# Attention one: layer-norm statistics and normalisation in four parts each, and the projections moved to later score banks

## The chip, the cores and the metric

The kernel runs on one core of one Trainium2 chip. The metric is the device time of one launch in microseconds (us).

## The reference

A two-layer tower over 8 x 1024 tokens with 256 channels: embedding, attention one, a mixture of four experts, a second attention, and a feed-forward layer quantised to four bits. The change touches attention one only:

```
h = h + attn(layernorm(h))
# attn, for each of 8 sequences of 1024 tokens and each of 16 heads of 16 channels
qkv  = x_head @ Wqkv + bqkv
att  = softmax((q @ k.T / 4) * tril(ones, -1))      # masked scores are 0, not -inf
out  = (att @ v) over all heads @ Wr + br
```

## The kernel before

Attention one (`attention_one`) takes the 8 sequences in two halves of 128 channels each, so 16 halves `hb`; a half has two groups (`gi` 0 and 1) of four heads. One turn of the loop is one half: a window of group 0 and a window of group 1. Each window computes 36 score banks (slots 0 to 35, event `S`): TensorE (PE) fills one of three PSUM banks `scoresT`, ScalarE (ACT) takes the exponential into `probs`, GpSimd (POOL) zeroes the masked triangle of some of them, and PE multiplies `probs` by `Vg` in six bursts (event `PV`, bursts 4 and 5 of a group run in the window after it).

All other work is hung on the slots by a table of positions, `AT[gi]`: `window()` puts each event behind a slot, and every engine walks the same list and runs what is its own. So the table sets the order of instructions on each in-order engine. The work that goes through PSUM uses a ring of four banks (`ring`): a use may be filled only when the use four places ahead of it has been read, by VectorE (DVE) or ACT (`bank_free`; for a pair of banks, both). The events are:

- `LN_STATS`, `LN_NORM`: DVE computes mean and variance of 8 token tiles (`st`, `mv`), POOL raises variance + eps to -1/2 (`rstd`, in `LN_NORM`), DVE writes the normalised `xn`. This is for the next half, once in a turn, in window 0.
- `XT`, `QK`, `MID`: PE transposes `xn`, ACT copies it (`xT`); PE projects to q and k in four banks; ACT reads each bank twice (`f32part`, and `parts` rounded to bf16), POOL subtracts, ACT copies the middle part (`MID`), POOL subtracts again (`parts_ok`). q and k are so split in three bf16 parts. In ACT's queue the copy of one `MID` stands ahead of the next `QK`.
- `V`, `VG`, `RSUM`, `SUF`, `TMP`, `EQ`, `PT`, `OM`, `OT`, `WR`: values, suffix sums for the masked part, division by the denominator, and the output projection, added to `h`.
- `MX`: the row maxima of the next group, 18 pairs of banks in a window. PE fills a pair, DVE reduces both. `CT` and the SP queue bring the result into `Qs`. The SP queue waits for `parts_ok` before it loads `Qm`, `Km` (`LOAD_MAX`) and then `stage` (`LOAD`).

Of the kernel before, what the change touches and what calls it, by code (L numbers as in the profile page):

```python
# [22 lines left out]
TPB = S // P  # L23
# [28 lines left out]
FUTURE = -2.0 ** 126  # L52
SCORE_BANKS, RING_BANKS = 3, 4
PROBS = 16


def score_slots():
# [20 lines left out]
def buffer(slot):  # L78

    return slot % PROBS if slot < 2 * PROBS else slot - 2 * PROBS + HPG  # L80

# [41 lines left out]
def wait_apart(eng, *waits):  # L123


    values = [value if isinstance(value, int) else eng.to_reg(value) for _, value in waits]
    if not all(isinstance(value, int) for value in values):
        eng.wait_ge(waits[0][0], 1)
    for (sem, _), value in zip(waits, values):
        eng.wait_ge(sem, value)  # L130
# [4 lines left out]


AT = {
    0: {"LN_STATS": 1, "LN_NORM": 3, "XT": 7, "PV_COPY": 4, "EQ": 6, "TMP": 0, "PT": 5, "OT": 24, "WR": 25, "RSUM": 5, "SUF": 12, "QK": (11, 13, 18, 20), "MID_LAG": 2, "V": 21, "VG": 5, "LOAD": 0, "MX": 2, "MX_END": 32, "MX_CURVE": 1.0, "PV_HALF": 14},
    1: {"PV_COPY": 4, "EQ": 6, "TMP": 0, "PT": 5, "WR": 1, "V": 8, "VG": 6, "LOAD": 0, "MX": 1, "MX_END": 32, "MX_CURVE": 1.0, "PV_HALF": 14},
    "V_IN": 0, "WR_IN": 1,  # L140
}
ALONE = {"LN_STATS": 0, "LN_NORM": 1, "XT": 2, "QK": (8, 9, 10, 11), "MID_LAG": 1, "V": 12, "PV_COPY": 1, "TMP": 2, "PT": 5, "OT": 11,
         "WR": 14, "VG": 14, "LOAD": 14, "MX": 15, "MX_END": 35, "MX_CURVE": 1.0}


def window(gi, ot, wr, tail, prologue, v, scores, following, load_max=False):


    others = {}
    pos_of = AT[gi] if scores else ALONE  # L150

    def at(pos, *events):
        others.setdefault(min(pos, UNITS - 1), []).extend(events)

    if prologue:
        at(pos_of["LN_STATS"], ("LN_STATS",))
        at(pos_of["LN_NORM"], ("LN_NORM",))
        at(pos_of["XT"], ("R", "XT", "act", 0), ("R", "XT", "act", 1))
    if tail:
        at(0, ("PV", -1, 4))  # L160
        at(3 if scores else 0, ("PV", -1, 5))
        at(pos_of["PV_COPY"], ("PV_COPY", -1, 1))
        at(pos_of["TMP"], ("TMP", -1))
        at(pos_of["PT"], ("R", "PT", "dve", -1, 0))
        at(pos_of["PT"] + 2, ("R", "PT", "dve", -1, 1), ("OM", -1))
    if ot:
        at(pos_of["OT"], ("R", "OT", "act", 0), ("R", "OT", "act", 1))
    if wr:
        for j in range(4):
            at(pos_of["WR"] + (j // 2 if scores else 0), ("R", "WR", "dve", j))  # L170
    if gi == 0 and scores:
        at(pos_of["RSUM"], ("RSUM",))
        at(pos_of["SUF"], ("R", "SUF", "dve", 0), ("R", "SUF", "dve", 1))
    if prologue:
        for n in range(4):
            at(pos_of["QK"][n], ("R", "QK", "act", n // 2, n % 2))
            at(pos_of["QK"][n] + pos_of["MID_LAG"], ("MID", n // 2, n % 2))
    if v:
        at(pos_of["V"], ("R", "V", "dve", 0), ("R", "V", "dve", 1))
    if following:  # L180
        at(pos_of["VG"], ("VG",))
        at(pos_of["LOAD"], ("LOAD",))
        if not scores:
            at(pos_of["LOAD"], *(("LOAD_FIRST", p) for p in range(PAIRS_MX)))
        uses = []
        for p in range(PAIRS_MX):
            for k in range(MAX_BANKS):
                uses.append([("R", "MX", "dve", 2 * p, k), ("R", "MX", "dve", 2 * p + 1, k)])
                if p and k == 4:
                    uses[-1] += [("R", "CT", "dve", p - 1)]  # L190
            uses[-1] += [("MAX_FINAL", p)] + ([("LOAD_MAX", p)] if load_max else [])
        lo, hi = pos_of["MX"], pos_of["MX_END"]
        for n, u in enumerate(uses):
            at(int(lo + (hi - lo) * (n / len(uses)) ** pos_of["MX_CURVE"]), *u)
        at(UNITS - 1, ("R", "CT", "dve", PAIRS_MX - 1))
    if scores:
        at(pos_of["EQ"], ("EQ",))
        at(pos_of["PV_HALF"], ("PV_COPY", 0, 0))
    events = []
    for pos in range(UNITS if scores else max(others, default=-1) + 1):  # L200
        if scores:
            events.append(("S", pos))
            events += [("PV", 0, b) for b, last in BURST_AT.items() if last == pos]
        events += others.pop(pos, [])
    return [(gi,) + e for e in events]
# [15 lines left out]
def plan():  # L221
    v1, wr1 = bool(AT["V_IN"]), bool(AT["WR_IN"])
    sections = {
        "init": window(1, False, False, False, True, True, False, True, True),
        "first": window(0, False, False, False, True, not v1, True, True, True) + window(1, False, False, True, False, v1, True, True, True),
        "loop": window(0, True, not wr1, True, True, not v1, True, True, True) + window(1, False, wr1, True, False, v1, True, True, True),
        "last": window(0, True, not wr1, True, False, False, True, True) + window(1, False, wr1, True, False, False, True, False),
        "final": window(0, True, True, True, False, False, False, False),
    }
    out, at = {}, (0, 0, 0)  # L230
    for name in ("init", "first", "loop", "last", "final"):
        out[name], end = number(sections[name], at)
        per = tuple(b - a for a, b in zip(at, end))
        out[name + "/per"] = per
        at = tuple(a + (HALVES - 2) * p for a, p in zip(at, per)) if name == "loop" else end
    assert out["loop/per"][0] % RING_BANKS == 0
    return out


def attention_one(nc, dram, h, shared):  # L240
    plans = plan()
    with ExitStack() as ctx:
        def sb(name, shape, dt=F32):
            return ctx.enter_context(nc.sbuf_tensor(name, shape, dt))

        def sem(name):
            return ctx.enter_context(nc.semaphore(name))
# [29 lines left out]
        Vg = sb("Vg", [P, 2, TPB, HPG, 32])  # L277
        probs = sb("probs", [P, PROBS, 512])
        cand = sb("cand", [P, 2, TPB, 9])
# [11 lines left out]
        OT = sb("OT", [P, S])  # L291
# [9 lines left out]
        mv_ok, rstd_ok, xn_ok = sem("mv_ok"), sem("rstd_ok"), sem("xn_ok")  # L301
        rest_ok, mid_ok, parts_ok = sem("rest_ok"), sem("mid_ok"), sem("parts_ok")
        stats_c, rs_c, rsum_c, rsum_ok = sem("stats_c"), sem("rs_c"), sem("rsum_c"), sem("rsum_ok")
# [53 lines left out]
        with nc.Block() as block:  # L357
# [68 lines left out]
            def _(pool):  # L426
# [16 lines left out]
                def gather(t, s):  # L443
                    nc.gpsimd.indirect_dma_start(h[:, t, :], None, dram["WT"],
                                                 bass.IndirectOffsetOnAxis(ap=tok[:, t:t + 1], axis=0)).then_inc(s, 16)
# [17 lines left out]
                def run(section, hb, it):  # L463
                    num = numbers(section, it)
                    for e in plans[section]:
                        gi, kind = e[0], e[1]
                        G = 2 * hb + gi
                        if kind == "S":
# [8 lines left out]
                                                        pattern=[[0, 2], [1, P]], channel_multiplier=-1).then_inc(mask_ok, 1)  # L477
                            if section == "first" and gi * UNITS + slot < TILES - TPB:
                                gather(TPB + gi * UNITS + slot, gat1)
                        elif kind == "LN_NORM":  # L480
                            wait_apart(pool, (mv_ok, hb + 2))
                            nc.gpsimd.tensor_scalar(rstd[:], mv[:, :, 1], EPS, None, ALU.add).then_inc(rs_c, 1)
                            pool.wait_ge(rs_c, hb + 2)
                            nc.gpsimd.tensor_tensor(rstd[:], rstd[:], minus_half[:], ALU.pow).then_inc(rstd_ok, 1)
# [22 lines left out]
                        elif kind == "MAX_FINAL":  # L507
                            g, par, n = G + 1, (gi + 1) % 2, PAIRS_MX * (G + 1) + e[2]
# [20 lines left out]
                        elif kind == "OM":  # L529
# [3 lines left out]
                            for j in range(2):  # L533
                                pool.wait_ge(rd_ok, 2 * g + j + 1)
                                t = slice(4 * j, 4 * j + 4)
# [58 lines left out]
            def _(dve):  # L594
# [3 lines left out]
                def run(section, hb, it):  # L598
                    num = numbers(section, it)
                    for e in plans[section]:  # L600
                        gi, kind = e[0], e[1]
                        G = 2 * hb + gi
                        g, nxt = G + 1, (gi + 1) % 2
                        hn = hb + 1
                        if kind == "LN_STATS":
                            if section == "init":
                                dve.wait_ge(gat0, 16 * TPB)
                            elif section == "loop":
                                dve.wait_ge(gat1, 16 * (TILES - TPB))
                            for t in range(TPB):  # L610
                                ins = nc.vector.bn_stats(st[:, t, :], h[:, TPB * (hn // 2) + t, :])
                            ins.then_inc(stats_c, 1)
                            wait_apart(dve, (stats_c, hn + 1))
                            for t in range(TPB):
                                ins = nc.vector.bn_aggr(mv[:, t, :], st[:, t, :])
                            ins.then_inc(mv_ok, 1)
                        elif kind == "LN_NORM":
                            dve.wait_ge(rstd_ok, hn + 1)
                            for t in range(TPB):
                                nc.vector.tensor_scalar(xn[:, t, :], h[:, TPB * (hn // 2) + t, bass.ds(P * (hn % 2), P)],  # L620
                                                        mv[:, t, 0:1], rstd[:, t:t + 1], ALU.subtract, ALU.mult).then_inc(xn_ok, 1)
                        elif kind == "VG":
# [11 lines left out]
                        elif kind == "R" and e[3] == "dve":  # L634
# [13 lines left out]
                            elif e[2] == "V":  # L648
                                if section != "init":
                                    dve.wait_ge(rsum_ok, hb + 1)  # L650
                                j = e[4]
                                nc.vector.tensor_tensor(Vh[:, 4 * j:4 * j + 4, :], src[:].rearrange("p (t n) -> p t n", t=4),
                                                        b_v[:, None, :].broadcast_to([P, 4, P]), ALU.add).then_inc(read_dve, 1)
                            elif e[2] == "SUF":
                                wait(dve, tmp_ok, 2 * hb)
                                j = e[4]
                                nc.vector.tensor_copy(suf[:, 4 * j:4 * j + 4, :, 0:HE],
                                                      src[:].rearrange("p (t h e) -> p t h e", t=4, h=8)).then_inc(read_dve, 1)
                            elif e[2] == "PT":
                                j = e[5]  # L660
                                dve.wait_ge(tmp_ok, G)
                                wait(dve, o_ok, 2 * (G - 1))
                                t = slice(4 * j, 4 * j + 4)
# [4 lines left out]
                            elif e[2] == "WR":  # L668
                                j = e[4]
# [1170 lines left out]
```

## Time and profile before

| | us |
|---|---|
| median of 3 runs | 3014.7 (3010.32 to 3017.59) |
| profiled execution, its own time | 3005.2 |
| its span | 3002.8 |
| one turn of attention one's loop (822.70 to 911.60) | 88.90 |
| window of group 0 in it / window of group 1 | 51.20 / 37.70 |
| PE busy in the turn | 76.25 |
| DVE / ACT / POOL busy in the turn | 62.11 / 50.16 / 33.88 |

Times in a view are from the start of the span. The loop has 14 turns, and the half ahead of it has the same window 0, so what changes in one window 0 counts 15 times. A gap in front of an instruction is shown with what ended it. The granted clock PEclk is 1.00 at 2.4 GHz and 0.50 at 1.2 GHz; a figure between is a mean over a stretch.

### The profile page before, as it was taken

What the parts mean: (1) busy time and instruction counts of PE and PEld (TensorE: products, weight loads), DVE (VectorE), ACT (ScalarE), POOL (GpSimd) and SP (SyncE); (2) the same over time, 40 slices, a digit from 0 to 9 for tenths busy, and PEclk for the clock granted to TensorE, in tenths of its full rate; (3) what the DMA queues carried; (4) which work ended last, traced back from release to release, by engine and by line L of the source; (5) the groups of instructions that cost most, each with busy time, mean ns of one, the idle gap of its engine ahead of it and who ended that gap; (6) DMA issues with size and microseconds to landing.
All of it is one profiled execution on the core that took longest, in us unless ns stands there. A gap on an engine that the chain in (4) does not pass through costs nothing. (4 is left out here: it accounts for less than half of the span.)

```text
span 3002.8 us, 58475 instructions
## 1 busy us (share of the span) xinstructions
PE 2581.3 (86%) x15254; PEld 1510.3 (50%) x15318; DVE 2118.6 (71%) x5668; ACT 1523.5 (51%) x3246; POOL 1640.4 (55%) x2564
## 2 busy tenths in 40 slices
PE   1778988888988888888868999898998979999999
PEld 0323433333333333343345666666666647666666
DVE  2657766777766767676567999898888965556554
ACT  1345555555555655555513655555555634444444
POOL 3664343333334333334245877777776757777675
PEclk7679999999999999999969999999999979999999
DMA  3353343344343344334230000000000000000000
GB/s 56 89 116 62 52 63 54 52 70 69 51 63 56 53 59 70 58 54 63 36 137 1 1 1 1 1 1 1 1 1 1 1 3 16 16 14 16 16 16 18
DMA packets 81300, 113.27 MB, mean 38 GB/s; under 512 B 25100, under 2 KB 37144, under 8 KB 80536
## 3 DMA queue, kind: packets, MB, share of 16 engines
q1 hardware_dynamic: 76360, 101.44, 19.8%
q0 software_dynamic: 3072, 8.39, 1.0%
q10 hardware_dynamic: 1744, 2.16, 0.2%
q14 instruction: 92, 0.75, 0.1%
q8 instruction: 32, 0.52, 0.1%
HBM read 18.98 MB, written 8.39 MB: 9 GB/s over the span
## 5 line engine op out<-in xcount | busy, mean ns | idle before, releaser
L554 ACT ACTIVATE probs<-scoresT 128x512 f32<-128x512 f32 x1152 | 639.7, 604 | 632.4 <-PE scoresT L697 622.9
L643 DVE TENSOR_REDUCE cand<-ring 128x4 f32<-128x512 f32 x1152 | 724.1, 680 | 219.6 <-PE ring L753 167.3
L476 POOL TENSOR_SCALAR_AFFINE_SELECT probs<-probs 128x256 f32<-128x256 f32 x512 | 204.9, 414 | 468.5 <-ACT probs L554 462.4
L697 PE MATMUL scoresT<-stage 98*128 98x512 bf16 (+3 forms) x1536 | 410.3, 344 | 22.2 <-ACT probs L554 16.6
L753 PE MATMUL ring<-Km,Qm 64*128 64x512 bf16 (+2 forms) x1792 | 253.0, 321 | 160.5 <-DVE cand L643 130.5
L717 PE MATMUL pv<-probs,Vg 128*32 128x512 f32 (+3 forms) x3072 | 325.2, 545 | 28.3 <-POOL probs L476 25.9
L753 PEld LDWEIGHTS ring<-Km,Qm 64*128 64x128 bf16 x1792 | 83.5, 95 | 375.6 <-DVE cand L643 239.5
L1180 PE MATMUL mm<-w_W,hT 128*128 128x256 f32 x1024 | 259.1, 399 | 8.7 <-ACT z L1268 2.8
L1200 PE MATMUL mm<-w_W,x2T 128*128 128x512 f32 x512 | 242.4, 596 | 0.3 <-DVE x L1419 0.2
L697 PEld LDWEIGHTS scoresT<-stage 98*128 98x128 bf16 x1536 | 114.5, 99 | 234.4 <-issue 139.1
L1261 ACT ACTIVATE hT<-mmT,w_be,w_g 128x128 f32<-128x128 f32 x512 | 185.5, 469 | 90.7 <-PE mmT L1191 90.7
L1180 PEld LDWEIGHTS mm<-w_W,hT 128*128 128x128 f32 x1024 | 207.1, 202 | 36.4 <-issue 0.3
L1622 PE MATMUL down_ps<-q_down,turned 128*128 128x256 f32 (+1 forms) x768 | 201.5, 396 | 2.3 <-ACT turned L1652 2.3
L1676 POOL TENSOR_TENSOR val<-val,power 128x960 f32<-128x960 f32 (+2 forms) x68 | 129.0, 1898 | 113.0 <-ACT power L1663 113.0
L717 PEld LDWEIGHTS pv<-probs,Vg 128*32 128x32 f32 x3072 | 85.5, 115 | 191.9 <-issue 154.7
L1584 PE MATMUL gate<-q_w_gate,turned 128*128 128x352 f32 x512 | 174.0, 462 | 0.7 <-ACT turned L1647 0.5
L1584 PE MATMUL up<-q_w_up,turned 128*128 128x352 f32 x512 | 173.0, 460 | 0.0
L1622 PEld LDWEIGHTS down_ps<-q_down,turned 128*128 128x128 f32 (+1 forms) x768 | 134.9, 189 | 68.2 <-issue 43.4
L1635 ACT ACTIVATE act_g<-gate 128x352 f32<-128x352 f32 x128 | 59.3, 463 | 208.9 <-PE gate L1584 202.5
L1328 POOL TENSOR_TENSOR u<-z,w_g 128x512 f32<-128x512 f32 x128 | 160.2, 1272 | 1.7 <-ACT z L1268 1.7
L1268 ACT ACTIVATE z<-mm,nmw,rw 128x256 f32<-128x256 f32 x256 | 124.0, 571 | 48.1 <-POOL nmw L1345 47.8
L1200 PEld LDWEIGHTS mm<-w_W,x2T 128*128 128x128 f32 x512 | 98.2, 192 | 87.5 <-issue 83.3
(254 smaller groups left out, 5280.9 us busy)
## 6 DMA issues: line engine op xcount, KB each, us to landing
stage<-parts SPq DMA_DIRECT2D x256, 96.0 KB, 2.8
stage<-parts SPq DMA_DIRECT2D x256, 64.0 KB, 2.8
Qm<-parts SPq DMA_DIRECT2D x128, 128.0 KB, 2.6
Km<-parts SPq DMA_DIRECT2D x128, 128.0 KB, 2.7
stage<-parts SPq DMA_DIRECT2D x256, 32.0 KB, 2.4
out<-result SPq DMA_DIRECT2D x64, 128.0 KB, 1.7
stage<-ct SPq DMA_DIRECT2D x128, 4.0 KB
w_W<-in_W SPq DMA_DIRECT2D x4, 512.0 KB
```

What stands on the lines that cost most here:

```text
L476: nc.gpsimd.affine_select(out=d, in_=d, compare_op=ALU.is_gt, fill=0.0, base=0, pattern=[[0, 2], [1, P]], channel_multiplier=-1).then_inc( ...
L554: nc.scalar.activation(probs[:, buffer(slot), :], scoresT[slot % SCORE_BANKS][:], ACT.Exp, scale=SOFT).then_inc(exp_ok, 1)
L643: ins = nc.vector.tensor_reduce(c, src[:].rearrange("p (t a b) -> p t a b", t=c.shape[1], b=P), AX.X, ALU.max)
L697: ins = nc.tensor.matmul(scoresT[slot % SCORE_BANKS][:, at:at + hi - lo], Ks[0:ROWS, gi, hh, P * kt:P * kt + P], Qs[0:ROWS, gi, hh, lo:hi] ...
L717: ins = nc.tensor.matmul(pv[32 * hh:32 * hh + 32, lo:512], Vg[:, par, kt, hh, :], probs[:, buffer(slot), column:column + 512 - lo], start= ...
L753: ins = nc.tensor.matmul(out[x][:, P * at:P * (at + n)], Qm[half[x], hh // 2, P * i:P * i + P], Km[half[x], hh // 2, P * j:P * (j + n)], s ...
L1180: ins = nc.tensor.matmul(o, hT[:, 2 * e + c, :], w["W2"][:, c, e, :], start=False, stop=(e % 2 == 1 and c == 1))
L1200: ins = nc.tensor.matmul(mm1[p][:], x2T[same][:, c, :], w["W1"][:, c, 2 * p:2 * p + 2, :].rearrange("p e n -> p (e n)"), start=False, stop ...
L1261: nc.scalar.activation(hT[:, j, :], mmT[p][:, P * k:P * k + P], ACT.Relu, bias=w["be1"][:, j:j + 1], scale=w["g1"][:, j:j + 1]).then_inc(h ...
L1328: nc.gpsimd.tensor_tensor(u[same][:, 2 * p:2 * p + 2, :], z[same][:, 2 * p:2 * p + 2, :], w["g2"][:].rearrange("p (e n) -> p e n", e=E4)[: ...
L1584: ins = nc.tensor.matmul(out[:, 0:HALF], turned[par][:, 5 + c, :], wt[:, c, HALF * a:HALF * a + HALF], start=(c == 0), stop=(c == 1))
L1622: ins = nc.tensor.matmul(down[:, 0:D], turned[1 - u][0:rows, at, :], w["down"][0:rows, k, :], start=(n == 0), stop=(n == CHUNKS - 1))
```

## The change

`LN_STATS` and `LN_NORM` become four events each, of two tiles. In window 0 the statistics stand behind slots 0, 2, 4 and 6 and the normalisations behind 10, 11, 12 and 13. POOL's power is an event of its own, `LN_POWER`, behind slot 6; it waits for all four statistics. The two transposes `XT` stand behind 13 and 15, the projections `QK` behind 16, 18, 20 and 22 with their `MID` two later, `V` behind 24, `RSUM` and `SUF` behind 3 and 9, and the maxima begin one slot earlier. In window 1 the four `WR` banks stand behind 2, 4, 6 and 8 and no longer two by two behind 1 and 2. The arithmetic is the same.

```diff
+LN_PARTS = 4
+LN_TILES = TPB // LN_PARTS
 AT = {
-    0: {"LN_STATS": 1, "LN_NORM": 3, "XT": 7, "PV_COPY": 4, "EQ": 6, "TMP": 0, "PT": 5, "OT": 24, "WR": 25, "RSUM": 5, "SUF": 12, "QK": (11, 13, 18, 20), "MID_LAG": 2, "V": 21, "VG": 5, "LOAD": 0, "MX": 2, "MX_END": 32, "MX_CURVE": 1.0, "PV_HALF": 14},
-    1: {"PV_COPY": 4, "EQ": 6, "TMP": 0, "PT": 5, "WR": 1, "V": 8, "VG": 6, "LOAD": 0, "MX": 1, "MX_END": 32, "MX_CURVE": 1.0, "PV_HALF": 14},
+    0: {"LN_STATS": (0, 2, 4, 6), "LN_NORM": (10, 11, 12, 13), "XT": (13, 15), "PV_COPY": 4, "EQ": 6, "TMP": 0, "PT": 5, "OT": 24, "WR": 25, "RSUM": 3, "SUF": 9, "QK": (16, 18, 20, 22), "MID_LAG": 2, "V": 24, "VG": 5, "LOAD": 0, "MX": 1, "MX_END": 32, "MX_CURVE": 1.0, "PV_HALF": 14},
+    1: {"PV_COPY": 4, "EQ": 6, "TMP": 0, "PT": 5, "WR": 2, "V": 8, "VG": 6, "LOAD": 0, "MX": 1, "MX_END": 32, "MX_CURVE": 1.0, "PV_HALF": 14},
...
-        at(pos_of["LN_STATS"], ("LN_STATS",))
-        at(pos_of["LN_NORM"], ("LN_NORM",))
-        at(pos_of["XT"], ("R", "XT", "act", 0), ("R", "XT", "act", 1))
+        for n in range(LN_PARTS):
+            at(pos_of["LN_STATS"][n], ("LN_STATS", n))
+            at(pos_of["LN_NORM"][n], ("LN_NORM", n))
+        at(pos_of["LN_STATS"][-1], ("LN_POWER",))
+        for n in range(2):
+            at(pos_of["XT"][n], ("R", "XT", "act", n))
...
-            at(pos_of["WR"] + (j // 2 if scores else 0), ("R", "WR", "dve", j))
+            at(pos_of["WR"] + (2 * j if scores else 0), ("R", "WR", "dve", j))
...
-                        elif kind == "LN_NORM":
-                            wait_apart(pool, (mv_ok, hb + 2))
+                        elif kind == "LN_POWER":
+                            wait_apart(pool, (mv_ok, LN_PARTS * (hb + 2)))
...
-                            for t in range(TPB):
+                            part = range(LN_TILES * e[2], LN_TILES * e[2] + LN_TILES)
+                            for t in part:
                                 ins = nc.vector.bn_stats(st[:, t, :], h[:, TPB * (hn // 2) + t, :])
                             ins.then_inc(stats_c, 1)
-                            wait_apart(dve, (stats_c, hn + 1))
-                            for t in range(TPB):
+                            wait_apart(dve, (stats_c, LN_PARTS * hn + e[2] + 1))
+                            for t in part:
                                 ins = nc.vector.bn_aggr(mv[:, t, :], st[:, t, :])
```

The first place is DVE's queue at the start of window 0. The rows are those of the half ahead of the loop, where there is no `PT` bank (in the loop `acc` and `rden` stand beside `Vg` too, and once more behind the fourth pair); `cand<-ring` is the reduction of one bank of maxima. Before:

```order
L611 BN_STATS st<-h 128x6 x8
L615 BN_AGGR mv<-st 128x2 x8
L643 TENSOR_REDUCE cand<-ring2 128x4
L643 TENSOR_REDUCE cand<-ring3 128x4
L620 TENSOR_SCALAR xn<-h,mv,rstd 128x128 x8
L643 TENSOR_REDUCE cand<-ring0 128x4
L643 TENSOR_REDUCE cand<-ring1 128x4
L628 COPY Vg<-Vh 128x32x16
L643 TENSOR_REDUCE cand<-ring2 128x4
L643 TENSOR_REDUCE cand<-ring3 128x4
```

Now:

```order
L617 BN_STATS st<-h 128x6 x2
L621 BN_AGGR mv<-st 128x2 x2
L649 TENSOR_REDUCE cand<-ring2 128x4
L649 TENSOR_REDUCE cand<-ring3 128x4
L617 BN_STATS st<-h 128x6 x2
L621 BN_AGGR mv<-st 128x2 x2
L649 TENSOR_REDUCE cand<-ring0 128x4
L649 TENSOR_REDUCE cand<-ring1 128x4
L617 BN_STATS st<-h 128x6 x2
L621 BN_AGGR mv<-st 128x2 x2
L649 TENSOR_REDUCE cand<-ring2 128x4
L649 TENSOR_REDUCE cand<-ring3 128x4
```

The eight statistics and the eight normalisations no longer stand around the first pair of maxima: one quarter of the statistics stands ahead of each of the first four pairs of maxima, and the normalisations (further down) follow the copies of the suffix sums, two quarters ahead of the seventh pair and two ahead of the eighth.

The second place is PE's queue at the second projection bank (L771 before, L777 now), again in the half ahead of the loop, where ring numbers differ from the loop's but distances don't. Before, behind it:

```order
L771 MATMUL ring1<-xT,w_qkv 128x512 [waits ring_read_act,ring_read_dve]
L753 MATMUL ring2<-Km,Qm 128x256 [waits ring_read_dve]
L753 MATMUL ring3<-Km,Qm 128x256
L739 MATMUL ring2<-future2,ident2 128x128
L739 MATMUL ring3<-future2,ident2 128x128
...
L697 MATMUL scoresT2<-stage 128x512 [waits exp_ok]
L697 MATMUL scoresT0<-stage 128x512 [waits exp_ok]
L739 MATMUL ring0<-future2,ident2 128x512 [waits ring_read_act,ring_read_dve]
```

Now, from the first projection bank on:

```order
L777 MATMUL ring0<-xT,w_qkv 128x512 [waits ring_read_act,ring_read_dve]
L759 MATMUL ring1<-Km,Qm 128x512 [waits ring_read_dve,max_in1]
L759 MATMUL ring2<-Km,Qm 128x512
L703 MATMUL scoresT2<-stage 128x512 [waits exp_ok]
L703 MATMUL scoresT0<-stage 128x512 [waits exp_ok]
L777 MATMUL ring3<-xT,w_qkv 128x512 [waits ring_read_act]
L759 MATMUL ring0<-Km,Qm 128x512 [waits ring_read_dve,ring_read_act]
L759 MATMUL ring1<-Km,Qm 128x512
L745 MATMUL ring0<-future2,ident2 128x128
L745 MATMUL ring1<-future2,ident2 128x128
...
L703 MATMUL scoresT1<-stage 128x512 [waits exp_ok]
L759 MATMUL ring2<-Km,Qm 128x512 [waits ring_read_act,ring_read_dve]
```

Between the first and the second projection bank the suffix sums (L781 and L783) and a pair of maxima stood before; now there are one pair of maxima and two score banks. The last pair shown in the second fence is the second pair behind the second projection bank, and its bank `ring3` is the one that this projection filled.

## Rows read from the trace of the kernel before

**Rows 1.** Length; busy PE, PEld, DVE, ACT, POOL; clock; DMA: window 0, window 1, turn.

```profile
822.70:873.90 51.20, 42.86 (x320) 20.23 (x320) 34.68 (x72) 29.18 (x55) 23.34 (x42) 0.90 0.33 50
873.90:911.60 37.70, 33.40 (x267) 13.74 (x267) 27.43 (x50) 20.98 (x40) 10.54 (x27) 0.95 0.47 73
822.70:911.60 88.90, 76.25 (x587) 33.97 (x587) 62.11 (x122) 50.16 (x94) 33.88 (x68) 0.92 0.39 60
```

**Rows 2.** PE timeline, window 0: start, us, instruction, idle before and its releaser.

```profile
822.70 0.39 PE L697 MATMUL scoresT<-stage 98*128 98x512 bf16 x1 [0.54 <-ACT probs L554]
823.39 3.21 PE L717 MATMUL pv<-probs,Vg 128*32 128x512 f32 x16 [0.30 <-POOL probs L476]
...
829.39 0.60 PE L791 MATMUL ring<-ident,pvS 128*128 128x128 f32 x4
835.95 0.61 PE L753 MATMUL ring<-Km,Qm 64*128 64x512 bf16 x2 [5.96 <-DVE cand L643]
...
837.32 1.91 PE L767 MATMUL ring<-ident,xn 128*128 128x128 f32 x8
...
841.39 1.71 PE L717 MATMUL pv<-probs,Vg 128*32 128x512 f32 x16
```

**Rows 3.** DVE timeline, the same stretch.

```profile
822.87 2.71 DVE L611 BATCH_NORM_STATS2 st<-h 128x6 f32 x8 [0.46 <-issue]
825.69 0.64 DVE L615 BATCH_NORM_AGGREGATE mv<-st 128x2 f32<-128x6 f32 x8
827.62 1.29 DVE L643 TENSOR_REDUCE cand<-ring 128x4 f32<-128x512 f32 x2 [1.29 <-PE ring L753]
831.43 3.87 DVE L620 TENSOR_SCALAR xn<-h,mv,rstd 128x128 f32 x8 [2.52 <-POOL rstd L484]
...
836.41 0.42 DVE L664 TENSOR_TENSOR acc<-ring,tmp 128x272 f32<-128x272 f32 x1
836.87 0.25 DVE L667 RECIPROCAL rden<-acc 128x16 f32<-128x16 f32 x1
...
840.77 2.41 DVE L643 TENSOR_REDUCE cand<-ring 128x4 f32<-128x512 f32 x4
```

**Rows 4.** PE's clock in 6 us stretches of window 0.

```profile
822.00:828.00 6.00, 5.16 (x33) 0.72 0.57 99
...
834.00:840.00 6.00, 4.05 (x18) 0.50 0.82 102
```

**Rows 5.** POOL timeline: the power, and a projection's first subtraction.

```profile
829.46 1.68 POOL L484 TENSOR_TENSOR rstd<-rstd,minus_half 128x8 f32<-128x8 f32 x1
...
857.33 1.17 POOL L488 TENSOR_TENSOR f32part<-f32part,parts 128x512 f32<-128x512 f32 x1 [0.72 <-ACT parts L572]
```

**Rows 6.** ACT timeline around one projection bank and its middle part.

```profile
855.92 0.76 ACT L571 ACTIVATE f32part<-ring,b_q 128x512 f32<-128x512 f32 x1
...
857.06 1.17 ACT L554 ACTIVATE probs<-scoresT 128x512 f32<-128x512 f32 x2
858.53 0.63 ACT L580 ACTIVATE parts<-f32part 128x512 bf16<-128x512 f32 x1 [0.30 <-POOL f32part L488]
```

**Rows 7.** PE timeline: suffix sums, score bank, projection, two holes (window 1's last).

```profile
845.98 0.49 PE L781 MATMUL ring<-Vh,upper 128*128 128x128 f32 x2
...
849.96 0.39 PE L697 MATMUL scoresT<-stage 98*128 98x512 bf16 x1
850.19 1.02 PE L771 MATMUL ring<-xT,w_qkv 128*128 128x512 f32 x2
...
852.72 0.60 PE L739 MATMUL ring<-future,ident 64*128 64x512 bf16 x4 [0.53 <-ACT parts L572]
...
865.59 0.38 PE L697 MATMUL scoresT<-stage 98*128 98x512 bf16 x1
...
887.76 0.39 PE L753 MATMUL ring<-Km,Qm 64*128 64x512 bf16 x2 [0.88 <-DVE cand L643]
```

**Rows 8.** SP queue, window 0: the first load that waits for `parts_ok`.

```profile
865.12 0.59 SPq L412 DMA_DIRECT2D Qm<-parts  x1
```

More of the change, by code:

```diff
@@ L137 @@
 AT = {
-    0: {"LN_STATS": 1, "LN_NORM": 3, "XT": 7, "PV_COPY": 4, "EQ": 6, "TMP": 0, "PT": 5, "OT": 24, "WR": 25, "RSUM": 5, "SUF": 12, "QK": (11, 13, 18, 20), "MID_LAG": 2, "V": 21, "VG": 5, "LOAD": 0, "MX": 2, "MX_END": 32, "MX_CURVE": 1.0, "PV_HALF": 14},
-    1: {"PV_COPY": 4, "EQ": 6, "TMP": 0, "PT": 5, "WR": 1, "V": 8, "VG": 6, "LOAD": 0, "MX": 1, "MX_END": 32, "MX_CURVE": 1.0, "PV_HALF": 14},
+    0: {"LN_STATS": (0, 2, 4, 6), "LN_NORM": (10, 11, 12, 13), "XT": (13, 15), "PV_COPY": 4, "EQ": 6, "TMP": 0, "PT": 5, "OT": 24, "WR": 25, "RSUM": 3, "SUF": 9, "QK": (16, 18, 20, 22), "MID_LAG": 2, "V": 24, "VG": 5, "LOAD": 0, "MX": 1, "MX_END": 32, "MX_CURVE": 1.0, "PV_HALF": 14},
+    1: {"PV_COPY": 4, "EQ": 6, "TMP": 0, "PT": 5, "WR": 2, "V": 8, "VG": 6, "LOAD": 0, "MX": 1, "MX_END": 32, "MX_CURVE": 1.0, "PV_HALF": 14},
     "V_IN": 0, "WR_IN": 1,
 }
-ALONE = {"LN_STATS": 0, "LN_NORM": 1, "XT": 2, "QK": (8, 9, 10, 11), "MID_LAG": 1, "V": 12, "PV_COPY": 1, "TMP": 2, "PT": 5, "OT": 11,
+ALONE = {"LN_STATS": (0, 0, 0, 0), "LN_NORM": (1, 1, 1, 1), "XT": (2, 2), "QK": (8, 9, 10, 11), "MID_LAG": 1, "V": 12, "PV_COPY": 1, "TMP": 2, "PT": 5, "OT": 11,
          "WR": 14, "VG": 14, "LOAD": 14, "MX": 15, "MX_END": 35, "MX_CURVE": 1.0}
@@ L618, in run @@
                             dve.wait_ge(rstd_ok, hn + 1)
-                            for t in range(TPB):
+                            for t in range(LN_TILES * e[2], LN_TILES * e[2] + LN_TILES):
                                 nc.vector.tensor_scalar(xn[:, t, :], h[:, TPB * (hn // 2) + t, bass.ds(P * (hn % 2), P)],
```

## The prediction

> **What bounds the kernel now.** I read the busy time of one turn first. PE is busy 76.25 of 88.90 us, DVE 62.11, ACT 50.16, POOL 33.88 [rows 1], so PE sets the pace wherever it isn't held up. In window 0 it is idle 51.20 - 42.86 = 8.34 us, in window 1 4.30. PE's timeline shows where: one hole of 5.96 us, ended by DVE's reduction of a ring bank [rows 2], beside 0.54 ahead of slot 0 and 0.30 behind it, 0.53 behind ACT's read of a projection bank [rows 2, 7], and small ones. DVE's timeline tells what the hole is made of. Statistics take 2.71 + 0.64; then comes one pair of maxima; then DVE stands 2.52 waiting for POOL's power of 1.68 [rows 5], and normalises for 3.87; the next pair of maxima is read only behind that [rows 3]. The ring has four banks, so PE can't run ahead. The view of the clock adds a second loss: behind the hole PE gets 0.50, half speed, from 834 to 840 [rows 4]. It did about 4.2 us of work there, which is 2.1 at full speed: the eight transposes took 1.91 where four take 0.60 at full speed [rows 2], so 0.7 of the 2.1 is theirs. The change can win at most 5.96 + 2.1 = 8.1 us in a turn, over 15 turns 121 us.
>
> **The new order, laid out by hand.** t is the time from slot 0's first matmul (822.70 before). Prices: a score bank 0.22, a projection 0.95 (0.86 to 1.02), all suffix sums 3.55 (from 845.98 to the score bank that follows the last pair of maxima, less that pair) [rows 7]; a burst 1.65, four transposes 0.60 [rows 2]; filling a pair of maxima 0.32 (0.39 less its overlap with what follows [rows 7]), and 0.11 more, an estimate, where four matmuls of a mask go with it. On DVE a pair costs 1.25 (four banks 2.41 to 2.5), `acc` with `rden` 0.65, two normalisations 3.87 / 4 = 0.97, a quarter of the statistics 0.68 + 0.16 + two waits on its own semaphore of about 0.1 (the gap between 825.58 and 825.69), so 1.05 [rows 3]. Four quarters are 4.2 instead of 3.46: 0.7 more DVE time.
>
> First stretch, slots 0 to 9. The burst at slot 0 still runs until t = 3.9 at half clock [rows 2, 4], so the first pair of maxima reaches DVE at 4.6; the first quarter of statistics is hidden ahead of it, and the other three aren't. From there DVE has four pairs, three quarters, `acc` and `rden` and `Vg`: 5.0 + 3.15 + 0.65 + 0.35 = 9.15, with no gap, until 13.75. PE has only 4 us of work in the same stretch, and needs banks that DVE frees one by one. By `bank_free` it waits 0.6 for the second pair's bank, 1.5 for the third's, 2.05 for the fourth's. POOL's power waits for the fourth quarter (t = 12.5) and ends at 14.5; the mask of slot 7 is queued behind it, and the burst at slot 9 waits for that mask: 0.85 more, until t = 15.0. So 5.0 of holes stand where 5.96 stood.
>
> Second stretch, slots 9 to 16. Burst and suffix sums keep PE until 20.2; DVE idles for 3 us there, since nothing is filled for it. Then the suffix copies, a pair, two quarters of normalisation, a pair and two more quarters are DVE's, and PE stands 1.55 at the first `XT` (needs tile 4 normalised) and 1.45 at the second (its ring bank is read behind the last quarter). The second half of the maxima starts at t = 30.0, with three projections still to do where before there were two.
>
> Third stretch, the projections. The chain through a bank is ACT's two reads 1.3 (855.92 to 857.25), POOL's subtraction 1.17, ACT's middle copy 0.63, and the next bank's two reads 1.3 [rows 5, 6]; with three semaphores of 0.1 it is 4.65 from filling one bank to freeing the next, since `MID` of one stands ahead of `QK` of the next in ACT's queue. POOL is free for it only behind the small operations of `MAX_FINAL`, which end just in time. PE's work between is three or four score banks, a projection and two pairs: 2.6. Between the first and second projection that leaves a hole of 2.05, and between the third and fourth, up to the bank of `OT`, 1.95. Before, slots 11 to 13 had the suffix sums between, and the chain cost 0.53 [rows 7]. Before the third a burst covers it.
>
> Sum of window 0: slot 25 comes at t = 45.4, and was at 865.59 - 822.70 = 42.9 [rows 7]: 2.5 us later. In holes it is 5.0 + 3.0 + 4.0 = 12.0, against 5.96 + 2.1 + 0.53 and 0.9 of small ones (8.34 less 5.96, 0.53 and 0.30 leaves 1.55 in window 0, of which I take 0.9 to lie ahead of slot 25). Behind slot 25 nothing changes. The SP queue gets `parts_ok` at about t = 46, before at 42.4 [rows 8], 7 us ahead of slot 0 of window 1; its loads then run some 3 us late and cost nothing while the next window's first maxima are later than that; without this cover it would be up to 3.
>
> Window 1: PE's first maxima now come ahead of `WR` and DVE starts 1.2 us earlier, but the four pairs and four `WR` are the same DVE work (5.0 + 2.7) and my walk brings the burst at slot 9 at 14.8, where it was 14.7; the hole of 0.88 [rows 7] stays as 0.9. Taken as 0, bounds -0.9 and +0.9.
>
> Clock: this is all at full speed behind t = 3.9. A stretch in which PE works a third of the time precedes the burst at slot 9, as before the hole preceded the half speed, so I take one burst at half speed again: +1.65. Bounds: 0 if the clock stays full, and +1.65 more behind each of the two projection holes.
>
> Here the Trainium skill bears on the sum (TensorE: Matmul & The Clock Gate, "HAM oscillation — how this bites in real kernels"): only long PE-idle gaps lower the clock. No new hole passes 2.1 us, so by it the +1.65 would fall away. The trace speaks against taking it so: the clock fell at slot 0 [rows 4], with no hole over 0.54 around it [rows 2]. The same page's "A second HAM failure mode: psum-queue depth-cycling" says that many micro-idles between groups of matmuls are enough to make the clock swing, which speaks against this change.
>
> Total: 2.5 + 1.65 = 4.15 a turn, times 15, is 62; 1 for the quarters ahead of the loop. The profiled execution took 3005.2, so 3068 by it; it ran 9.5 below the median of the runs shown, and against that median it is 3078.
>
> **Rivals.**
> *Faster.* DVE catches up in its 3 us under the suffix sums: if a pair is ready for it there, the two `XT` holes (3.0) vanish and holes are 9.0 (gain 0.5 a turn), and if ACT's reads also overlap so that the projection holes halve, 2.5: 2977 to 3007. For it: PE is the busiest engine and its largest hole is removed. Against: the order fills no pair between the burst at slot 9 and the last suffix sum. It decides when new holes and half-clock loss together come below 9.5 a turn. 0.20.
> *No change.* Holes add up to the old ones, 3009 to 3021: 0.10.
> *Slower, clock full throughout* (the long-gap mechanism): 15 x 2.5 = 38, 3053: 0.20. Here every new hole is below 2.1 and no stretch behind slot 9 shows 0.50.
> *Slower, clock swings behind each hole* (the micro-idle mechanism): 15 x (4.15 + 3.3) = 112, 3127: 0.10.
> *Forecast*, one half-speed stretch, 3055 to 3105: 0.40.
>
> **How the numbers follow.** A difference of 0.2% (6 us) is what can be told from none. Slower is 0.40 + 0.20 + 0.10 = 0.70, same 0.10, faster 0.20. The range reaches from 2988, within the faster case, to 3128; about 0.12 lies below and 0.06 above.
>
> **What the changed profile would show.** DVE without its 2.52 wait for `rstd`; PE's hole of 5.96 gone, and between slots 4 and 9 three or four holes of 0.6 to 2.1 ended by DVE, one of under 1 ended by POOL; holes of 1 to 2 ahead of both `XT`; two holes of about 2 behind projections, ended by ACT's `parts`; ACT's middle copy waiting for POOL's subtraction. Window 0 would be about 55 us, window 1 37.7. The forecast is wrong if window 0 is under 51: then DVE's queue isn't the bound of slots 1 to 16, or the chain of projections is shorter than 4.65. It is wrong the other way if `Qm` and `stage` come late and slot 0 of window 1 waits for them.

## The result, and the profile after

The changed kernel takes 3041.61 us (median of 4 runs, 3040.99 to 3044.24), the kernel before 3013.88 in the same comparison: ratio 1.0096, 95% interval 1.0080 to 1.0112. It is slower, as forecast, but by 28 us and not by the forecast 63. The two profiled executions lie 37 us apart, since the one of the kernel before ran 9 us below its median.

The two profiles say at once that this number is a difference of two large ones. These are windows of the changed kernel's span (length, DVE's busy time, clock, DMA): attention one up to its last addition to `h`, then the experts and attention two together, from the first `x2T` to the last `h<-both`, then the rest.

```profile
0.00:1603.40 1603.40, 977.30 (x1953) 0.88 0.37 61
1672.60:2459.10 786.50, 747.65 (x2919) 0.98 0.00 0
2459.10:3039.70 580.60, 333.96 (x695) 0.98 0.04 15
```

The same windows of the kernel before:

```profile
0.00:1524.40 1524.40, 997.68 (x1953) 0.91 0.38 64
1593.70:2423.50 829.80, 733.41 (x2919) 0.96 0.00 1
2423.50:3002.80 579.30, 333.66 (x695) 0.98 0.04 15
```

Attention one is 79 us longer. A stage of which the diff touches no line is 43 us shorter, with as many instructions (x2919) and DVE busy about as long.

**Window 0 after.** Its PE timeline in the turn from 962.8 to 1057 answers to [rows 2] and [rows 7]; columns as there, and `...` where rows are left out.

```profile
963.43 3.16 PE L723 MATMUL pv<-probs,Vg 128*32 128x512 f32 x16 [0.30 <-POOL probs L481]
...
970.39 0.65 PE L797 MATMUL ring<-ident,pvS 128*128 128x128 f32 x4 [0.32 <-DVE cand L649]
...
972.49 0.39 PE L759 MATMUL ring<-Km,Qm 64*128 64x512 bf16 x2 [1.24 <-DVE cand L649]
...
975.68 0.61 PE L759 MATMUL ring<-Km,Qm 64*128 64x512 bf16 x2 [1.43 <-DVE cand L649]
...
977.73 2.84 PE L723 MATMUL pv<-probs,Vg 128*32 128x512 f32 x16 [0.47 <-POOL probs L481]
...
990.01 0.66 PE L773 MATMUL ring<-ident,xn 128*128 128x128 f32 x4 [0.39 <-DVE cand L649]
...
996.54 0.39 PE L759 MATMUL ring<-Km,Qm 64*128 64x512 bf16 x2 [2.15 <-ACT parts L577]
...
997.18 3.56 PE L723 MATMUL pv<-probs,Vg 128*32 128x512 f32 x16
...
1006.28 1.09 PE L801 MATMUL ring<-ident,O 128*128 128x128 f32 x8 [1.74 <-ACT parts L577]
```

The hole of 5.96 is gone. In its place stand 0.32, 1.24 and 1.43 behind DVE and 0.47 behind POOL's mask, and further on 2.15 and 1.74 behind ACT's `parts`. PE's clock in the window and in three stretches of it (length, busy, clock), and last the stretch behind the 1.74 in the turn before:

```profile
962.80:1019.10 56.30, 47.09 (x321) 0.85 0.30 45
973.20:980.00 6.80, 4.90 (x23) 0.50 0.84 105
997.10:1000.50 3.40, 3.40 (x17) 0.50 0.00 0
1007.40:1010.80 3.40, 3.40 (x17) 0.50 0.00 0
914.50:917.80 3.30, 3.30 (x35) 1.00 0.00 0
```

So in this turn each of the two later holes has a stretch at half speed behind it, which window 0 before didn't have there; the whole window is 56.3 us and was 51.2 [rows 1]. The 2.15 has one in all 14 turns of the loop, the 1.74 only in every second.

Twelve turns of the loop together, from one `tmp` of POOL to that of 24 windows later, PE alone, before and after:

```profile
290.30:1355.20 1064.90, 913.91 (x7040) 0.93 0.39 59
307.70:1433.80 1126.10, 959.95 (x7040) 0.90 0.37 56
```

A turn takes 88.7 us before, 76.2 busy and 12.6 idle, and 93.8 after, 80.0 busy and 13.8 idle. The matmuls are as many, so of the 5.1 us that a turn grew only 1.3 are holes, and most of the 3.8 of busy time is the lower clock.

DVE and POOL in the turn from 962.8, against [rows 3] and [rows 5]:

```profile
985.95 1.11 DVE L626 TENSOR_SCALAR xn<-h,mv,rstd 128x128 f32 x4
```

```profile
975.21 0.25 POOL L487 TENSOR_SCALAR rstd<-mv 128x8 f32<-128x8 f32 x1 [1.47 <-DVE mv L621]
975.54 1.68 POOL L489 TENSOR_TENSOR rstd<-rstd,minus_half 128x8 f32<-128x8 f32 x1
977.18 0.41 POOL L481 TENSOR_SCALAR_AFFINE_SELECT probs<-probs 128x256 f32<-128x256 f32 x1
```

POOL waits 1.47 for the last quarter of the statistics, and slot 7's mask goes behind the power, as laid out. But four normalisations take 1.11, 0.26 each from start to start, where eight took 3.87.

ACT's chain at the projections, against [rows 6]:

```profile
994.70 0.63 ACT L585 ACTIVATE parts<-f32part 128x512 bf16<-128x512 f32 x1 [0.29 <-POOL f32part L493]
995.23 0.67 ACT L576 ACTIVATE f32part<-ring,b_q 128x512 f32<-128x512 f32 x1
995.80 0.68 ACT L577 ACTIVATE parts<-ring,b_q 128x512 bf16<-128x512 f32 x1
```

ACT stands for POOL's subtraction, copies the middle part, and only then reads the second bank, until 996.48; PE resumes at 996.54.

**The experts' stage.** DVE's waits over some 40 tiles in the kernel before, from 1780 to 2300 (total, times, longest), show two that no engine's work ended:

```profile
DVE gy L1378 <- issue: 24.8, 10, 2.6
DVE both L1382 <- issue: 21.0, 10, 2.3
```

Once in each pass of that loop, which takes four tiles, DVE stands idle in two places without a wait that the profile shows, 4.6 us together; a tile there takes 15.6 us, from one write of `h` to the next, where the others take mostly 12.0. The stage has 11 such passes. The DMA view of the same stretch (1780 to 2300) has one queue at work:

```profile
q14 instruction: 51, 0.42, 0.3%
```

In the changed kernel's stretch of that length the queue has 1 packet, and every tile takes 12.0 or 12.1. The packets are of 8192 bytes. The experts' loop in DVE's code lies seven instructions further on in the changed kernel, since the statistics in parts add seven to DVE's share of attention one's loop. So the place of DVE's code is the first theory to test.

### The profile page after: what moved, and what is told of

Same layout as the page of the kernel before. It is cut to its first block and busy times, and to the rows that moved or that the text cites. A ratio compares the mean times of both kernels' runs of the same rounds, so it can differ in the third digit from the quotient of the medians.

```text
span 3039.7 us, 58573 instructions
## 1 busy us (share of the span) xinstructions
PE 2618.4 (86%) x15254; PEld 1498.5 (49%) x15318; DVE 2112.8 (70%) x5668; ACT 1537.9 (51%) x3246; POOL 1641.1 (54%) x2564
## 5 line engine op out<-in xcount | busy, mean ns | idle before, releaser
L703 PE MATMUL scoresT<-stage 98*128 98x512 bf16 (+3 forms) x1536 | 422.7, 345 | 28.3 <-ACT probs L559 17.5
L723 PE MATMUL pv<-probs,Vg 128*32 128x512 f32 (+3 forms) x3072 | 366.2, 603 | 38.9 <-POOL probs L481 24.9
L1186 PE MATMUL mm<-w_W,hT 128*128 128x256 f32 x1024 | 243.1, 380 | 8.1 <-ACT z L1274 3.3
L517 POOL CAST c<-m 128x16 bf16<-128x16 f32 x64 | 12.7, 198 | 372.0 <-DVE m L639 372.0
L1186 PEld LDWEIGHTS mm<-w_W,hT 128*128 128x128 f32 x1024 | 195.8, 191 | 31.2
L1274 ACT ACTIVATE z<-mm,nmw,rw 128x256 f32<-128x256 f32 x256 | 123.8, 565 | 56.6 <-POOL nmw L1351 56.3
```

What stands on the lines that cost most here:

```text
L703: ins = nc.tensor.matmul(scoresT[slot % SCORE_BANKS][:, at:at + hi - lo], Ks[0:ROWS, gi, hh, P * kt:P * kt + P], Qs[0:ROWS, gi, hh, lo:hi] ...
L723: ins = nc.tensor.matmul(pv[32 * hh:32 * hh + 32, lo:512], Vg[:, par, kt, hh, :], probs[:, buffer(slot), column:column + 512 - lo], start= ...
L1186: ins = nc.tensor.matmul(o, hT[:, 2 * e + c, :], w["W2"][:, c, e, :], start=False, stop=(e % 2 == 1 and c == 1))
```

## The experiments

Ratios are to the kernel before, run beside each, with their 95% interval. The diffs of the table show the entries that change and not the whole line. The code of DVE has the same length ahead of the experts' loop in all kernels built on the changed one, except `after_pad121`, and in those with seven memsets. In the profiles of all of them the stage takes 784 to 787 us; in the kernel before, `before_rsum8` and `after_pad121` it takes about 830.

**Where DVE's code lies.** `before_pad7` is the kernel before with

```diff
+        pad = sb("pad", [P, 7])
...
                 sections(dve, run)
+                for i in range(7):
+                    nc.vector.memset(pad[:, i:i + 1], 0.0)
```

> The kernel before, with seven one-column memsets on DVE behind its share of attention one, as many instructions as the change adds to DVE's code ahead of the experts' loop. Theory (place of DVE's code): the 3.6 us that the experts' loop loses once in four tiles go, 11 times, so 3014 - 40 = 2974 us, attention one unchanged at 88.9 us a turn. Rival (the new order of attention one shortens the experts' stage in another way): 3014 us, the 3.6 us stay.

Measured 2968.45 us, 0.9851 (0.9835 to 0.9868). The stage (DVE's window), and the instruction queue from 1790 to 2300:

```profile
1602.00:2385.70 783.70, 747.43 (x2919) 0.99 0.00 0
```

```profile
q14 instruction: 1, 0.01, 0.0%
```

`after_pad121` is the changed kernel with 121 such memsets at the same place:

```diff
+        pad = sb("pad", [P, 121])
...
+                for i in range(121):
+                    nc.vector.memset(pad[:, i:i + 1], 0.0)
```

> The changed kernel, with 121 one-column memsets on DVE behind its share of attention one, which with the seven instructions of the change make 128. Theory (place of DVE's code, in blocks of 8192 bytes as the instruction queue's packets are): the loss of 3.6 us in four tiles comes back, 40 us, and the memsets cost some 8, so 3041 + 48 = 3089 us. Rival (new order): 3041 + 8 = 3049 us.

Measured 3087.62 us, 1.0253 (1.0236 to 1.0270). The stage:

```profile
1675.10:2505.30 830.20, 733.66 (x2918) 0.96 0.00 1
```

783.7 and 830.2 against 829.8 before and 786.5 after: the stage's length follows the place of DVE's code and not the order of attention one. Both expectations hold: seven instructions more take the loss away, 128 bring it back. Other counts were not tried. The memsets cost less than the 8 us allowed. Seven instructions of no use make the kernel before 44 us faster. So at equal place of the code the change costs 3041.6 / 2968.5, the ratio of ratios being 1.0249: 73 us. By the profiles it is 71: the stage begins at 1602.0 here and at 1672.6 in the changed kernel.

**The projections' chain.** `after_qk3` spaces them three slots apart:

```diff
-"QK": (16, 18, 20, 22)
+"QK": (16, 19, 22, 25)
```

> The changed kernel, with the projections behind slots 16, 19, 22 and 25 and no longer two slots apart. Theory (chain ACT, POOL, ACT through a bank): the holes of 2.16 and 1.74 us in front of PE shrink below 0.7 each, and with them the half clock behind them, 3 to 5 us a turn, 2966 to 2996 us. Rival (DVE or the later inputs are the bound there, and the wait moves): within 10 us of 3041.

Measured 2982.04 us, 0.9907 (0.9890 to 0.9923), 60 us less than the changed kernel. PE's timeline, at the projections and at slot 0 of window 1:

```profile
871.49 0.39 PE L759 MATMUL ring<-Km,Qm 64*128 64x512 bf16 x2 [0.85 <-ACT parts L577]
...
878.93 1.09 PE L801 MATMUL ring<-ident,O 128*128 128x128 f32 x8 [0.41 <-ACT parts L577]
...
892.82 0.60 PE L703 MATMUL scoresT<-stage 98*128 98x512 bf16 x1 [1.36 <-DMA stage<-ct]
```

The holes shrink to 0.85 and 0.41, the first to a little more than the 0.7 expected, and one of 0.60 stands behind the fourth projection, which now comes later. PE's clock is 1.00 from 871.5 to 886, past all three. The last row is new: with the last `MID` behind slot 27 the SP queue is late and slot 0 waits 1.36 for it. The projections can't be pushed back at will.

`qk_alone` puts only this end of the change on `before_pad7`:

```diff
-"QK": (11, 13, 18, 20), "V": 21, "MX": 2
+"QK": (16, 18, 20, 22), "V": 24, "MX": 1
```

> The kernel before with seven memsets on DVE (2968 us), and of the change only its end: projections behind 16, 18, 20 and 22, V behind 24, maxima one slot earlier; statistics and normalisations stay in one piece where they were. Theory (the chain through the projection banks is what costs): two holes of about 2 us ended by ACT's parts, each with half clock behind it, 4 to 5 us a turn, about 3030 us. Rival (the cost comes from the statistics and normalisations in parts): below 2980 us.

Measured 3026.66 us, 1.0067 (1.0050 to 1.0084); against 0.9851 that is 65 us, if the two comparisons are set side by side. Its PE timeline has the changed kernel's two holes to the hundredth:

```profile
981.23 0.46 PE L756 MATMUL ring<-Km,Qm 64*128 64x512 bf16 x2 [2.16 <-ACT parts L573]
...
990.92 1.30 PE L798 MATMUL ring<-ident,O 128*128 128x128 f32 x8 [1.74 <-ACT parts L573]
```

As expected. Most of the 73 us is this end of the change (projections, values and the earlier maxima, which were not taken apart). Here the hole of 5.96 is still there; so the parts of statistics and normalisation, which take it away in the changed kernel, win nothing on balance: a turn takes 93.4 us here and 93.8 there.

**The output projection in window 1.** `wr_alone` is `before_pad7` with `WR` of window 1 at 2, 4, 6 and 8:

```diff
-"WR": 1
+"WR": 2
...
-            at(pos_of["WR"] + (j // 2 if scores else 0), ("R", "WR", "dve", j))
+            at(pos_of["WR"] + (2 * j if scores else 0), ("R", "WR", "dve", j))
```

> The kernel before with seven memsets on DVE (2968 us), and of the change only the output projection's banks behind slots 2, 4, 6 and 8 of window 1. Theory (it costs what window 1 grew by, 0.84 us a turn): 2981 us. Rival (no cost, as forecast; window 1's 0.84 us come from what reaches it late out of window 0): 2968 us within 5.

Measured 2959.02 us, 0.9835 (0.9819 to 0.9852), at the lower end of the interval of `before_pad7`, and a turn takes 88.7 us as there. No cost: the first theory fell, the forecast's 0 held for `WR`.

**The price of a normalisation.** `before_rsum8` moves POOL's suffix additions:

```diff
-"RSUM": 5
+"RSUM": 8
```

> The kernel before, with POOL's suffix additions behind slot 8 and no longer behind slot 5. Theory (DVE's normalisations are slowed by POOL's additions, which read two SBUF operands at the same time): eight normalisations take about 2.1 us and no longer 3.87, PE's hole is 4.2 and no longer 5.96, a turn is 1.8 us shorter, 3014 - 27 = 2987 us. Rival (0.48 us is the price of one normalisation there, whatever POOL does): hole 5.96, 3014 us.

Measured 3002.63 us, 0.9964 (0.9951 to 0.9976): 11 us, not 27. DVE, then PE:

```profile
835.43 2.14 DVE L620 TENSOR_SCALAR xn<-h,mv,rstd 128x128 f32 x8 [2.41 <-POOL rstd L484]
```

```profile
838.22 0.61 PE L753 MATMUL ring<-Km,Qm 64*128 64x512 bf16 x2 [4.13 <-DVE cand L643]
```

The duration and the hole came as expected, 2.14 and 4.13; the time didn't. The clock took it. In the turn shown PE gets half speed for only half of the stretch behind slot 0, and the window shrinks by all of the 1.7; so it is in 3 of the loop's 14 turns. In the other 11, the next one among them, the hole is mostly 4.2, half speed lasts as long as before, and PE is at work in more of it. The stretch in the turn shown, and in the next:

```profile
834.70:841.50 6.80, 3.28 (x16) 0.75 0.82 104
923.20:930.00 6.80, 5.84 (x25) 0.50 0.82 102
```

and in the kernel before:

```profile
833.42:840.24 6.82, 4.29 (x20) 0.50 0.84 105
```

1.55 us more of the work runs at half speed in the next turn, some 0.8 us lost, which with the 0.8 to 0.9 by which a turn got shorter on average is about the 1.7 of the hole.

**Where the statistics stand.** `after_stats0` is the changed kernel with all four parts behind slot 0:

```diff
-"LN_STATS": (0, 2, 4, 6)
+"LN_STATS": (0, 0, 0, 0)
```

> The changed kernel with one entry of its table changed: all four quarters of the statistics, and so the power, behind slot 0. Theory (three quarters of the statistics were put out of DVE's idle time into its busiest stretch): the holes ahead of slot 9 shrink from about 3.5 to under 1.5 us and a turn by 2 to 4 us, 2985 to 3010 us. Rival (DVE bounds that stretch by the maxima anyway): 3035 us or more.

Measured 3007.15 us, 1.0011 (1.0002 to 1.0021), 0.85% under the changed kernel, some 26 us, and in the range of the theory. But the holes ahead of slot 9 didn't shrink as the theory had it. PE's waits for DVE's maxima and for POOL's masks over twelve turns (total, times, longest) are, in the changed kernel:

```profile
PE ring L759 <- DVE cand L649: 65.3, 72, 2.1
PE pv L723 <- POOL probs L481: 18.2, 36, 0.8
```

and in this one:

```profile
PE pv L723 <- POOL probs L481: 42.7, 36, 3.0
PE ring L759 <- DVE cand L649: 41.5, 62, 1.2
```

DVE's holes shrink by 2.0 us a turn, and POOL's grow by as much: the power now stands at the head of POOL's queue and waits for all statistics, so the additions of `Rsum` behind it run late, ahead of the masks for which the burst at slot 9 waits.

```profile
857.76 3.30 POOL L506 TENSOR_TENSOR Rsum<-Rsum,Vh 128x128 f32<-128x128 f32 x6
```

PE is idle 13.7 us in a turn, against 13.8, and busy 78.1 against 80.0. So nearly all of the gain came through the clock and not through fewer holes.

**Better orders.** `stats0_norm8` has the changed kernel's code, all statistics and the power behind slot 0, and

```diff
-"LN_NORM": (10, 11, 12, 13), "XT": (13, 15), "RSUM": 3, "SUF": 9, "QK": (16, 18, 20, 22)
+"LN_NORM": (8, 9, 10, 11), "XT": (11, 13), "RSUM": 4, "SUF": 12, "QK": (13, 16, 19, 22)
```

with `WR` as before the change.

> The changed kernel's code with another table: all statistics and the power behind slot 0, where DVE idles for over 3 us; normalisations in quarters behind 8 to 11 with no suffix addition beside them; XT 11 and 13, RSUM 4, SUF 12, projections 13, 16, 19 and 22 (three apart), output projection as before. Theory (the change lost by statistics out of DVE's idle time, by the chain, and by nothing else): the hole of 5.96 us and most of its half clock go with nothing in their place, 4 to 6 us a turn less than the kernel before at equal code place, 2880 to 2910 us. Rival (holes only move, DVE bounds slots 1 to 9 in any order): 2950 to 2970 us.

Measured 2927.30 us, 0.9733 (0.9716 to 0.9749): beyond the rival, but short of the theory. Three projection holes of 0.6 to 1.0 are left, and a larger one that the theory didn't have, behind POOL's additions. PE, then POOL:

```profile
823.83 2.65 PE L723 MATMUL pv<-probs,Vg 128*32 128x512 f32 x16 [2.59 <-POOL probs L481]
```

```profile
819.26 3.36 POOL L506 TENSOR_TENSOR Rsum<-Rsum,Vh 128x128 f32<-128x128 f32 x6
```

`stats0_norm4` is the same code with the normalisations four slots earlier, `RSUM` behind them, and transposes, projections and `V` earlier too; the diff is to `stats0_norm8`:

```diff
-"LN_NORM": (8, 9, 10, 11), "XT": (11, 13), "RSUM": 4, "SUF": 12, "QK": (13, 16, 19, 22), "V": 24
+"LN_NORM": (4, 5, 6, 7), "XT": (8, 10), "RSUM": 8, "SUF": 12, "QK": (11, 14, 18, 21), "V": 22
```

> As stats0_norm8, but normalisations behind 4 to 7, XT 8 and 10, RSUM 8, projections 11, 14, 18 and 21, V 22, near the positions of the kernel before. Theory (DVE is short only in slots 1 to 9, and idles beside the suffix sums): normalisations there bring back holes of 2 to 3 us, 1 to 3 us a turn worse than stats0_norm8. Rival (a normalisation of 0.26 us is small enough anywhere): equal within 8 us.

Measured 2913.91 us, 0.9688 (0.9672 to 0.9704). The hole ahead of the fourth pair came (2.31), yet the kernel is faster, not slower: the projections, further apart again, leave one hole of 1.09, and with `RSUM` behind slot 8 the hole of 2.59 behind POOL's mask is gone. Neither expectation held.

`norm4_rsum4` puts POOL's additions back beside the normalisations:

```diff
-"RSUM": 8
+"RSUM": 4
```

> As stats0_norm4, with POOL's suffix additions behind slot 4, so beside the normalisations, and no longer behind slot 8. Theory (contention of DVE's normalisations with POOL's additions): eight normalisations take 1 to 1.8 us longer, a turn about 1 us, 2925 to 2940 us. Rival (DVE has room for it there): 2914 us within 6.

Measured 2912.57 us, 0.9701 (0.9685 to 0.9718): the rival. The normalisations are slower again (484 ns on average, 413 in `stats0_norm4`), and the hole is 2.90, not 2.31, but the clock is at half speed for 3.4 us behind slot 0 of that window and not for 6.8 as in most turns there. So DVE had no room for it: PE is idle 0.6 us more in a turn, and what paid that back was the clock.

`stats0_norm6` is `stats0_norm4` with the last three normalisations two slots later, the first one slot:

```diff
-"LN_NORM": (4, 5, 6, 7), "RSUM": 8, "SUF": 12
+"LN_NORM": (5, 7, 8, 9), "RSUM": 9, "SUF": 13
```

> As stats0_norm4, with normalisations behind 5, 7, 8 and 9, RSUM 9 and SUF 13. Theory (the hole of 2.31 us ahead of the fourth pair of maxima is two quarters of normalisation in DVE's queue): the hole shrinks to about 1.5 us, 2900 to 2910 us. Rival (the wait moves to the transposes): 2914 us or more.

Measured 2863.97 us, 0.9540 (0.9524 to 0.9556), better than was expected of it, and the fastest here: 4.6% under the kernel before, 3.2% under it at equal place of the code. Its timeline has these holes from slot 1 on, up to the last slots; in most other turns the first is 1.74:

```profile
868.91 0.39 PE L759 MATMUL ring<-Km,Qm 64*128 64x512 bf16 x2 [1.47 <-DVE cand L649]
...
873.46 0.33 PE L773 MATMUL ring<-ident,xn 128*128 128x128 f32 x1 [0.15 <-DVE xn L626]
...
887.17 0.39 PE L759 MATMUL ring<-Km,Qm 64*128 64x512 bf16 x2 [1.09 <-ACT parts L577]
```

and the clock over window 0 behind its first burst, then over attention one:

```profile
866.00:906.00 40.00, 35.33 (x280) 1.00 0.34 54
100.00:1420.00 1320.00, 1161.05 (x9183) 0.96 0.42 67
```

In 13 of the loop's 14 turns the clock doesn't fall in the window's body, with largest holes of 1.47 to 1.91. In one it does, behind a hole of 1.74:

```profile
294.99 0.39 PE L759 MATMUL ring<-Km,Qm 64*128 64x512 bf16 x2 [1.74 <-DVE cand L649]
```

```profile
295.50:298.70 3.20, 3.20 (x16) 0.50 0.85 104
```

Against `stats0_norm4` PE is idle 1.2 us less in a turn and busy 2.2 less. That, and not the holes alone, is why the step gave 50 us.

**Turn by turn.** The same twelve turns in each profile, us in a turn; the matmuls are the same within a few records.

| kernel | turn | PE busy | PE idle |
|---|---|---|---|
| before | 88.7 | 76.2 | 12.6 |
| changed | 93.8 | 80.0 | 13.8 |
| `after_qk3` | 89.9 | 77.8 | 12.1 |
| `qk_alone` | 93.4 | 78.3 | 15.1 |
| `before_rsum8` | 87.9 | 76.7 | 11.2 |
| `after_stats0` | 91.8 | 78.1 | 13.7 |
| `stats0_norm8` | 86.0 | 74.6 | 11.4 |
| `stats0_norm4` | 85.4 | 75.6 | 9.8 |
| `norm4_rsum4` | 85.4 | 75.0 | 10.4 |
| `stats0_norm6` | 82.0 | 73.4 | 8.6 |

## Why the prediction was right or wrong

**The step that failed** is the last: "Total: 2.5 + 1.65 = 4.15 a turn, times 15, is 62". It sums attention one and takes every other stage as untouched, without a reason. Attention one's part was near: 63 forecast, and 73 at equal place of the code. The term that is missing is -43 us in the experts' loop, from seven added instructions that moved DVE's code; `before_pad7` and `after_pad121` show it from both sides. A hint of it was open to view ahead of the run: the kernel before had tiles of 15.6 us among tiles of 12.0 there, and DVE idle on "issue". Which way the change would move it couldn't be read there. I read only the stage that the diff touches.

**What bounds the kernel, and the gain it could have**: right. The hole of 5.96 went, and so did the 2.52 wait for `rstd`; and of the 8.1 us in a turn that an order could win at most, the best one here wins 6.8.

**Slots 0 to 9**: right in kind. Forecast 0.6, 1.5, 2.05 and 0.85, measured 0.32, 1.24, 1.43 (2.07 in the turn before) and 0.47. That three quarters of the statistics had been moved out of idle time is shown by `after_stats0` as far as DVE's holes go, 2.0 us in a turn; the net gain there came through the clock.

**Slots 9 to 16**: wrong in size. The two `XT` holes were forecast at 1.55 and 1.45, and are 0.27 ahead of a pair and 0.39 ahead of a transpose. The term mis-sized is "two normalisations 3.87 / 4 = 0.97"; they take 0.51 to 0.55. With two such terms ahead of each hole that is, by an estimate, 0.9 of the 1.1 to 1.3 us missing; the rest is open. `before_rsum8` shows the cause: in the kernel before, POOL's additions ran at the same time.

**The chain of projections**: right, 2.05 and 1.95 forecast, 2.15 and 1.74 measured, and `qk_alone` and `after_qk3` confirm the cause. In a turn `qk_alone` costs 4.6 us, 2.5 of it idle time of PE and 2.1 busy time at the lower clock; the sum had 4.0 of holes, for 0.53 before, and no clock of their own behind them.

**The clock**: wrong in size. One stretch at half speed was in the sum, 1.65. In the turn from 962.8 there are three behind slot 0, with 4.90, 3.40 and 3.40 us of work in them, so by an estimate 5.9 lost; in every second turn there are two. That is near the rival of the micro-idle mechanism. The holes of that window, on the other hand, add up to 8.0, where 12.0 were forecast. Over a turn the forecast had 4.6 us more of idle time (12.0 for 5.96, 0.53 and 0.9) and 0.45 less lost to the clock (1.65 for 2.1); measured are 1.3 more idle and 3.8 more busy. That these errors offset each other, and 4.15 came near the measured 5.1, was luck. The Trainium skill's rule that only long gaps lower the clock (TensorE: Matmul & The Clock Gate, "HAM oscillation — how this bites in real kernels") doesn't describe this kernel: the clock fell behind holes of 2.15 and 1.74 us. With the same page's "A second HAM failure mode: psum-queue depth-cycling", that many small gaps make the clock swing, the trace agrees.

**Window 1, and the SP queue**: 0 was right for `WR`. Window 1 as a whole grew by 0.8, from 36.9 to 37.7 on average over the twelve turns, inside the bounds of 0.9; in `wr_alone` it stays at 36.9, and what makes the 0.8 is open. The SP queue's cover held in the changed kernel; `after_qk3` shows its end, and the price of 1.36.

For the code's place the Trainium skill has a rule (Runtime: NRT & Kernel Launch, "Instruction fetch mechanics"): a taken branch to code that isn't in the engine's instruction memory any more waits for a fetch. The trace agrees as far as it goes, with about five packets of 8192 bytes in each pass of the loop or none. That the loop then spans one block too many is my reading; no run shows the blocks' bounds themselves.

## What to carry to other kernels

A change to code ahead of a loop moves that loop's place in the engine's code: compare stage by stage, and pad the code to equal length, before a difference of one or two per cent is put down to an order. Work that is cut in pieces is only better if the pieces still stand in idle time, and moving it can close one engine's hole and open another's, as POOL's mask showed. Work that goes through a ring of banks needs as much other work between two uses as the chain behind one bank takes. A hole of 2 us costs more than itself when the clock falls behind it; its size alone doesn't tell whether it will (1.74 did in some turns and not in others, and behind 2.90 the stretch was shorter than behind 2.31). So split a turn into idle time and busy time of the same work, and read both.

## What the runs showed of the hardware

- The experts' loop lost some 3.9 us in each of 11 passes of four tiles or nothing at all, on seven instructions of DVE's code ahead of it: 44 us of 3013.
- DVE's `tensor_scalar` on 128 x 128 fp32 takes 0.27 us from start to start with POOL's additions moved away, and 0.48 on average while POOL adds two SBUF operands (eight in 2.14 against 3.87).
- A hole shortened from 5.96 to 4.2 us gave back only half of its 1.7 in 11 of 14 turns: as long a stretch at half speed then held 5.84 us of PE's work, not 4.29. In the 3 turns in which the stretch was half as long, nearly all of it came back.
- As many matmuls took PE 73.4 us in a turn in the best order and 80.0 in the changed kernel. With no hole over 1.91 us there was no stretch at half speed in the body of window 0 in 13 of 14 turns.
